# Normalisation in the projection: epsilon added on GpSimd, row 3 normalised as one piece before row 1's softplus, row 1 loaded after the first weight pair

## The chip, the cores and the metric

The kernel runs on one core of a Trainium2 chip. Its time is the device time in microseconds (us) of one execution. The engines are TensorE (PE in the profile, its weight loads PEld), VectorE (DVE), ScalarE (ACT), GpSimd (POOL) and SyncE (SP), which here only starts transfers. Each engine has a program of its own that runs in order; they wait for each other through semaphores.

## What is computed

Four rows (batch elements) of 1024 tokens with 128 channels go through a state-space layer, a mixture of experts, a long convolution and the mixture again, each with a residual. The change lies in the state-space layer's first part:

```python
def _layernorm(x, axis=-1, eps=1e-05):
    m = jnp.mean(x, axis=axis, keepdims=True)
    v = jnp.var(x, axis=axis, keepdims=True)
    return (x - m) / jnp.sqrt(v + eps)

# state-space layer, on the normalised x
x_in = x @ w_in
proj = x_in @ w_x                                  # split into dt_low, B, C
dt = softplus(dt_low @ w_dt + b_dt) * (DT_MAX - DT_MIN) + DT_MIN
# scan over tokens t:  h = exp(dt*A)*h + (dt*A . B)*x_in ;  y = h . C + Dp*x_in
```

## The kernel before

The kernel is in stages; the first two matter here. `project` normalises the tokens, transposes them, multiplies them by folded weights and makes for each row the inputs of the scan. `scan` then runs, for each of the four rows, 16 scans of 128x1024 on VectorE (L786), with ScalarE making the decays ahead of each (L780) and GpSimd multiplying 15 of the 16 results by C (L924; the tenth is multiplied by VectorE). The mixtures and the convolution follow.

In `project` the unit of work is half a row, called (b, q): four tiles of 128 tokens of row b. For each half:

- SyncE loads x. Rows 0 and 1 come in halves (L249), rows 2 and 3 whole (L253). Between row 0 and row 1 SyncE waits until the three weights w_x, w_dt and b_dt have landed (`weights_in`). ScalarE has started five small transfers before: w_in and the identity, which count on `first_in`, and then those three.
- `statistics_of(b, q)` on VectorE: four `bn_stats` (L471), a drain, four `bn_aggr` (L474), which leave mean and variance, a drain, and one 128x4 `tensor_scalar` (L476), which adds epsilon to the variances and releases GpSimd.
- `deviation(b, q)` on GpSimd: one 128x4 `tensor_tensor` with the power -0.5 (L309), which gives 1/sqrt.
- `normalize(b, q)` on VectorE: four 128x128 `tensor_scalar` (L482), each (x - mean) * rstd from SBUF to SBUF.
- TensorE transposes the tiles (L605), ScalarE copies them out of PSUM (L349), TensorE multiplies them by four weights: the step's z (L613), u (L618), B (L625) and C (L632). ScalarE takes Abs of z (L356) and copies the others; VectorE's `positive(b, q)` (L489) takes max(z, 0) out of PSUM and so frees z's bank for the next half.

For each whole row, ScalarE makes ln(1 + exp(-|z|)) (L373, L377). VectorE's `softplus(b)` (L496) adds it to the positive part; both its inputs lie in SBUF. The step is then split into three bfloat16 parts: ScalarE casts the first (`first_part`, L382), GpSimd's `remainder(b)` (L305, 128x1024) subtracts it, ScalarE casts the second (L386), VectorE's `third_part(b)` (L508) takes the rest. VectorE's `step_times_u(b)` (L503, two SBUF inputs) makes dt*u, TensorE multiplies it by the rates (L642, `step_products`), and VectorE's `input_rows(b)` (L514) makes the scan's input. `rates()` (L525 to L530) makes the rates once, `constants()` (L518 to L521) the bfloat16 tables, `skip_diagonal()` (L535) a 128x128 `tensor_scalar` from SBUF to SBUF.

The order on every engine is written out by hand. VectorE's, from the middle: softplus(0), positive(1,0), statistics_of(3,0), statistics_of(3,1), constants, step_times_u(0), third_part(0), positive(1,1), normalize(3,0), rates, softplus(1), positive(2,0), normalize(3,1), step_times_u(1), skip_diagonal, positive(2,1), input_rows(0), third_part(1), softplus(2), and so on to the first scans. GpSimd's: six deviations, remainder(0), deviation(3,0), deviation(3,1), remainder(1), remainder(2). After normalize(0,1) VectorE also has a run of semaphore increments for the later stages (`more_credit`, L115).

Of the kernel before, what the change touches and what calls it, by code (L numbers as in the profile page):

```python
# [20 lines left out]
ALU = mybir.AluOpType  # L21
# [3 lines left out]
P = 128  # L25
# [18 lines left out]
EPS = 1e-5  # L44
# [148 lines left out]
def project(plan, ps, m, t):  # L193
# [22 lines left out]
    spread, rstd = sb("in_spread", [P, 2, HT]), sb("in_rstd", [P, 2, HT])  # L216
    m["scratch"] = scratch = sb("scratch", [P, 2 * SEQ])
    xn, xn_t = (scratch[:, i * SEQ:(i + 1) * SEQ].rearrange("p (q s) -> p q s", q=2) for i in range(2))
    a_neg = sb("a_neg", [P, STATES])
    a_range = sb("a_range", [P, P])  # L220
    a_p = sb("a_p", [P, GROUPS])
# [24 lines left out]
    @plan.on("sync")  # L246
    def _(sp):
        def half_row(b, q):
            sp.dma_start(x[:, b * BT + q * HT:b * BT + (q + 1) * HT, 0:D],  # L249
                         t["x"][b, q * HALF:(q + 1) * HALF, :].rearrange("(i p) d -> p i d", p=P)).then_inc(x_in[2 * b + q], 16)  # L250

        def row(b):
            sp.dma_start(x[:, b * BT:(b + 1) * BT, 0:D], t["x"][b, :, :].rearrange("(i p) d -> p i d", p=P)).then_inc(x_in[b + 2], 16)  # L253

        half_row(0, 0)
        half_row(0, 1)
        sp.wait_ge(weights_in, 16 * 3)
        half_row(1, 0)
        half_row(1, 1)
        row(2)  # L260
        sp.dma_start(const[:, P:], t["table"][:, P:]).then_inc(consts_in, 16)
        row(3)
        sp.dma_start(a_neg[:, :], t["a_A_log"]).then_inc(a_in, 16)
        sp.dma_start(a_p[:, :], t["a_A_log_p"]).then_inc(a_in, 16)
        sp.dma_start(m["skip"][:, :], t["a_Dp"].rearrange("(d o) -> d o", o=1)).then_inc(m["skip_in"], 16)
        sp.dma_start(m["w_r_raw"][:, :], t["f_Wr"]).then_inc(m["router_in"], 16)
        sp.dma_start(m["b_r"][:, :], t["f_br"].rearrange("(o e) -> o e", o=1).broadcast_to([P, EXPERTS])).then_inc(m["router_in"], 16)

        sp.wait_ge(zero_made, 1 + CREDIT)

        def clear(dst, b):
            sp.dma_start(dst[b * SEQ:(b + 1) * SEQ, :].rearrange("(p j) d -> p (j d)", p=P), zero[:, :]).then_inc(m["prepared"], 16)

        sp.dma_start(m["taps"][:, :], zero[0:1, 0:4 * P]).then_inc(m["prepared"], 16)
        for b in range(BATCH):

            if b < BATCH - 1:
                need(sp, lo_done, b + 1)
            else:
                need(sp, last_lo, 2)  # L280
            sp.dma_start(m["steps"][:, b * PARTS * SEQ:(b + 1) * PARTS * SEQ], part[:, :]).then_inc(steps_out, 16)
            sp.wait_ge(steps_out, b * 16 + 16)
            sp.sem_inc(parts_free, 1)
            for a in range(PARTS):
                sp.dma_start(stack[a * QUARTER:(a + 1) * QUARTER, :, b * SEQ:(b + 1) * SEQ],
                             m["steps"][:, (b * PARTS + a) * SEQ:(b * PARTS + a + 1) * SEQ].rearrange(
                                 "(q r) s -> r q s", r=QUARTER)).then_inc(stacked[b], 16)
        for dst in m["slots"]:
            for b in range(BATCH):
                clear(dst, b)  # L290
        sp.wait_ge(m["prepared"], PREPARED)
        need(sp, inp_done, BATCH)

    @plan.on("gpsimd")
    def _(pool):
        pool.memset(m["neg_half"][:, :], -0.5).then_inc(half_made, 1)
        pool.memset(m["ones"][:, :], 1.0)
        pool.memset(zero[:, :], 0.0).then_inc(zero_made, 1)
        pool.wait_ge(half_made, 1 + CREDIT)

        def remainder(b):

            pool.wait_ge(hi_done, b + 1 + CREDIT)
            need(pool, lo_done, b)
            pool.tensor_tensor(rest[:, :], sp_all[:, b * SEQ:(b + 1) * SEQ], part[:, 0:SEQ], ALU.subtract).then_inc(rest_done, 1)  # L305

        def deviation(b, q):
            pool.wait_ge(moments_done, 2 * b + q + 1 + CREDIT)
            pool.tensor_tensor(rstd[:, q, :], spread[:, q, :], m["neg_half"][:, 0:HT], ALU.pow).then_inc(rstd_done, 1)  # L309

        deviation(0, 0)
        deviation(0, 1)
        deviation(1, 0)
        deviation(1, 1)
        deviation(2, 0)
        deviation(2, 1)
        remainder(0)
        deviation(3, 0)
        deviation(3, 1)
        remainder(1)  # L320
        remainder(2)
        late["gpsimd"] = {0: lambda: (need(pool, dtu_done, BATCH), need(pool, lo_done, BATCH - 1))}
# [144 lines left out]
    def _(dve):  # L467
        def statistics_of(b, q):
# [2 lines left out]
                dve.bn_stats(stats[:, q, i, :], x[:, b * BT + q * HT + i, 0:D])  # L471
            dve.drain()
            for i in range(HT):
                dve.bn_aggr(moments[:, q, i, :], stats[:, q, i, :])  # L474
            dve.drain()
            dve.tensor_scalar(spread[:, q, :], moments[:, q, :, 1], EPS, None, ALU.add).then_inc(moments_done, 1)  # L476

        def normalize(b, q):
            dve.wait_ge(rstd_done, 2 * b + q + 1 + CREDIT)
# [79 lines left out]
        third_part(0)  # L559
        positive(1, 1)  # L560
        normalize(3, 0)
        rates()
        softplus(1)
        positive(2, 0)
        normalize(3, 1)
        step_times_u(1)
        skip_diagonal()
        positive(2, 1)
# [1711 lines left out]
```

## Time and profile before

| | us |
|---|---|
| median of 3 runs | 469.01 |
| lowest, highest | 466.15, 469.39 |
| the profiled execution's own time | 466.43 |
| its span, first to last instruction | 464.6 |
| VectorE busy in the span | 333.3 (72%) |
| GpSimd busy | 290.2 (62%) |
| TensorE busy | 350.6 (75%) |
| ScalarE busy | 232.9 (50%) |

Times in the profile count from the span's start. A row of a timeline gives start, duration, engine, line, operation, output<-inputs and the number of instructions merged into it; a bracket gives the idle time before it and what ended it. Two VectorE rows that follow without a wait overlap by about 0.08 us in such a view, so what an instruction costs its engine is the distance between two starts.

### The profile page before, as it was taken

To read this page: it belongs to the slowest core of one execution; us is meant where nothing else is said; L and a number is where in the kernel's file an instruction comes from. 1 tells how busy PE (TensorE), PEld (TensorE's weight loads), DVE (VectorE), ACT (ScalarE), POOL (GpSimd) and SP (SyncE) were. 2 spreads that over 40 slices of the span, in tenths; PEclk is the share of its full clock that TensorE was granted. 3 is DMA by queue.
4 is the path that set the end of the run, shared out by engine and by line. 5 is a ranking of instruction groups with operands and counts; after the bars stand their busy time and mean duration, and the time that the engine had idled before them with its cause. 6 is when DMAs were issued, how large, how long until landed. Compare 5 with 4: busy or idle time off the path is not lost.

```text
span 464.6 us, 5440 instructions
## 1 busy us (share of the span) xinstructions
PE 350.6 (75%) x1552; PEld 178.2 (38%) x1552; DVE 333.3 (72%) x772; ACT 232.9 (50%) x383; POOL 290.2 (62%) x203
## 2 busy tenths in 40 slices
PE   4988658769967957969574787287899677688792
PEld 3433213315313403424122554135666655344441
DVE  5999999999999999986433765353869845355341
ACT  3888856556556466533121495044796111346440
POOL 3331497999999999955744000867637565426755
PEclk9999968985967888897767799589599998699987
DMA  6214420784100100101313251111302121132201
GB/s 168 83 70 136 137 66 7 231 309 128 45 0 2 45 1 1 45 4 39 98 36 107 80 161 69 46 34 37 89 0 65 41 79 60 35 126 80 64 15 33
DMA packets 28826, 33.37 MB, mean 72 GB/s; under 512 B 5357, under 2 KB 20737, under 8 KB 28796
## 3 DMA queue, kind: packets, MB, share of 16 engines
q1 hardware_dynamic: 24428, 25.96, 18.0%
q0 software_dynamic: 3712, 6.84, 4.8%
q8 instruction: 13, 0.21, 0.2%
q10 hardware_dynamic: 656, 0.21, 0.2%
q14 instruction: 17, 0.14, 0.1%
HBM read 14.23 MB, written 19.65 MB: 73 GB/s over the span
## 4 chain that ended last, share of the span: by engine, by line
issue 26%; PE 26%; DVE 26%; ACT 9%; another core or an unknown queue 4%; DMA 3%; DVEq 3%; POOL 1%; ACTq 0%; SPq 0%; POOLq 0%
DVE states L786 14%; PE ps L1834 2%; ACT scaled L1393 2%; PE ps L1920 2%; PE ps L1345 2%; PE ps L1073 2%; PE ps L1613 2%; DVE scratch L482 2%; PE ps L153 2%; PE ps L1191 2%; PE ps L1329 1%; PE ps L1909 1%; ACT ps L780 1%; POOL x L1289 1%
## 5 line engine op out<-in xcount | busy, mean ns | idle before, releaser
L924 POOL TENSOR_TENSOR states<-states,c_rows 128x1024 f32<-128x1024 f32 x60 | 142.6, 2410 | 9.2 <-DVE dtu L503 5.1
L786 DVE TENSOR_TENSOR_SCAN states<-ps,inp 128x1024 f32<-128x1024 f32 x64 | 140.5, 2264 | 0.6 <-ACT ps L780 0.5
L780 ACT ACTIVATE ps<-ps,bias_p,scale_p 128x1024 f32<-128x1024 f32 x64 | 75.0, 1177 | 57.0 <-PE ps L774 57.0
L1165 POOL DMA_INDIRECT slots<-x,put x56 | 54.7, 977 | 43.8 <-DVE put L1159 28.8
L774 PE MATMUL ps<-stack,sel 96*128 96x512 bf16 x128 | 47.7, 466 | 28.9 <-DVE states L786 27.4
L1289 POOL DMA_INDIRECT x<-answers,put x28 | 27.3, 976 | 50.8 <-DMA answers<-reply 39.6
L1488 POOL DMA_INDIRECT out<-reply,home x32 | 31.8, 995 | 23.5 <-DVE reply L1465 15.9
L1465 DVE SCALAR_TENSOR_TENSOR reply<-ps,rows,kept 128x128 f32<-128x128 f32 x64 | 18.6, 344 | 26.4 <-remote 12.0
L808 PE MATMUL ps<-states,red 128*32 128x512 f32 x256 | 36.2, 673 | 0.2 <-POOL states L924 0.2
L774 PEld LDWEIGHTS ps<-stack,sel 96*128 96x128 bf16 x128 | 9.7, 107 | 64.8 <-DVE states L786 54.2
L1861 DVE SCALAR_TENSOR_TENSOR c_s<-c_u,c_w_tap,c_s 128x1024 f32<-128x1024 f32 (+1 forms) x20 | 20.6, 1068 | 13.0 <-ACT c_s L1851 11.4
L1008 DVE BATCH_NORM_STATS2 stats<-x 128x6 f32<-128x128 f32 x96 | 19.8, 279 | 10.8 <-DMA x<-answers,put 9.7
L1624 PE MATMUL ps<-d_hidden,w 128*128 128x512 f32 x32 | 21.0, 742 | 3.2 <-ACT d_hidden L1582 3.2
L1345 PE MATMUL ps<-w,hidden 128*128 128x128 f32 x112 | 16.2, 288 | 7.5 <-ACT hidden L1407 6.4
L1613 PE MATMUL ps<-d_rows_t,w 128*128 128x512 f32 x32 | 20.7, 735 | 1.5 <-ACT d_hidden L1582 0.8
L1582 ACT ACTIVATE d_hidden<-ps,b 128x512 f32<-128x512 f32 x16 | 11.0, 685 | 21.4 <-PE ps L1616 10.3
L153 PE MATMUL ps<-ones 128*128 128x512 bf16 x69 | 19.6, 431 | 2.2 <-POOL states L924 1.4
L305 POOL TENSOR_TENSOR rest<-states,part 128x1024 f32<-128x1024 f32 x3 | 6.5, 2178 | 20.6 <-ACT part L382 20.6
L1017 ACT ACTIVATE rstd<-moments,eps 128x8 f32<-128x8 f32 (+1 forms) x13 | 3.9, 298 | 30.8 <-DVE moments L1011 24.2
L1834 PE MATMUL ps<-c_xt,c_w_in 128*128 128x512 f32 x32 | 17.4, 670 | 2.1 <-ACT c_xt L1199 1.3
L1451 DVE SCALAR_TENSOR_TENSOR kept<-b,rows 128x128 f32<-128x128 f32 x64 | 18.2, 345 | 0.6
L1345 PEld LDWEIGHTS ps<-w,hidden 128*128 128x128 f32 x112 | 13.5, 191 | 12.7 <-ACT hidden L1407 10.3
(207 smaller groups left out, 675.7 us busy)
## 6 DMA issues: line engine op xcount, KB each, us to landing
slots<-zero SPq DMA_DIRECT2D x8, 528.0 KB
rows<-slots SPq DMA_DIRECT2D x16, 264.0 KB
steps<-part SPq DMA_DIRECT2D x4, 768.0 KB, 3.3
stack<-steps SPq DMA_DIRECT2D x12, 256.0 KB, 4.1
answers<-x SPq DMA_DIRECT2D x4, 512.0 KB, 3.2
answers<-reply SPq DMA_DIRECT2D x8, 256.0 KB, 3.2
out<-x SPq DMA_DIRECT2D x3, 512.0 KB
x<-in_x SPq DMA_DIRECT2D x4, 256.0 KB, 3.1
```

Source lines behind the costliest of these rows:

```text
L153: pe.matmul(bank(ps, at), m["ones"][:, :], ones, start=True, stop=True)
L774: last = pe.matmul(bank(ps, slot(b, u) + q), sel[0:PARTS * QUARTER, (g % QG) * P:(g % QG + 1) * P], stack[:, g // QG, bass.ds(b * SEQ + q ...
L780: act.activation(bank(ps, slot(b, u), 2), bank(ps, slot(b, u), 2), ACT.Exp, scale=m["scale_p"][:, group(u):group(u) + 1], bias=m["bias_p"] ...
L786: dve.tensor_tensor_scan(h[:, u * SEQ:(u + 1) * SEQ], bank(ps, slot(b, u), 2), inp[:, b * SEQ:(b + 1) * SEQ], 0.0, ALU.mult, ALU.add).then ...
L808: last = pe.matmul(ps[c * QUARTER:(c + 1) * QUARTER, (6 + q) * HALF:(7 + q) * HALF], red[:, r * QUARTER:(r + 1) * QUARTER], h[:, (QUARTERS ...
L924: eng.tensor_tensor(h[:, u * SEQ:(u + 1) * SEQ], h[:, u * SEQ:(u + 1) * SEQ], c_rows[:, b * SEQ:(b + 1) * SEQ], ALU.mult).then_inc(done, 1)
L1165: pool.indirect_dma_start(out=m["slots"][n // BATCH], out_offset=bass.IndirectOffsetOnAxis(m["put"][:, b, i:i + 1], 0), in_=m["x"][:, b * ...
L1289: pool.indirect_dma_start(out=m["x"][:, b * BT + i, 0:D], out_offset=None, in_=m["answers"], in_offset=bass.IndirectOffsetOnAxis(m["put"][ ...
L1345: last = pe.matmul(ps[:, at + j * D:at + (j + 1) * D], m["hidden"][:, e % 2, j * P:(j + 1) * P], m["w2"][:, e, :], start=True, stop=True)
L1488: pool.indirect_dma_start(out=m["out"], out_offset=bass.IndirectOffsetOnAxis(m["home"][:, e, j:j + 1], 0), in_=m["reply"][:, e, j * D:(j + ...
L1613: pe.matmul(at, self.m["w1"][:, e, :], self.rows_t[:, half], start=True, stop=False)
L1834: pe.matmul(bank(self.ps, self.U + s), self.w_in[:, s, :], self.xt[:, b % 2, h * HALF:(h + 1) * HALF], start=True, stop=True).then_inc(sel ...
```

## The change

1. The epsilon: `statistics_of` loses its second drain and the `tensor_scalar` of L476; the last `bn_aggr` releases GpSimd itself. `deviation` on GpSimd gets a 128x4 `tensor_tensor` add of the variances and a tile filled with epsilon, and a drain, ahead of the power. A 128x4 memset of that tile comes first in GpSimd's program.
2. VectorE's order: `normalize(3, 1)` stands directly behind `normalize(3, 0)`, ahead of `rates`, `softplus(1)` and `positive(2, 0)`.
3. SyncE starts row 1's loads once w_in and the identity have landed, and no longer waits for the three later weights.

```diff
+    in_eps = sb("in_eps", [P, HT])
...
-        sp.wait_ge(weights_in, 16 * 3)
+        sp.wait_ge(first_in, 16 * 2)
         half_row(1, 0)
...
+        pool.memset(in_eps[:, :], EPS)
         pool.memset(m["neg_half"][:, :], -0.5).then_inc(half_made, 1)
...
         def deviation(b, q):
             pool.wait_ge(moments_done, 2 * b + q + 1 + CREDIT)
+            pool.tensor_tensor(spread[:, q, :], moments[:, q, :, 1], in_eps[:, :], ALU.add)
+            pool.drain()
             pool.tensor_tensor(rstd[:, q, :], spread[:, q, :], m["neg_half"][:, 0:HT], ALU.pow).then_inc(rstd_done, 1)
...
             for i in range(HT):
-                dve.bn_aggr(moments[:, q, i, :], stats[:, q, i, :])
-            dve.drain()
-            dve.tensor_scalar(spread[:, q, :], moments[:, q, :, 1], EPS, None, ALU.add).then_inc(moments_done, 1)
+                last = dve.bn_aggr(moments[:, q, i, :], stats[:, q, i, :])
+            last.then_inc(moments_done, 1)
...
         normalize(3, 0)
+        normalize(3, 1)
         rates()
         softplus(1)
         positive(2, 0)
-        normalize(3, 1)
         step_times_u(1)
         skip_diagonal()
```

## Rows read from the trace of the kernel before

**Rows 1.** Busy time by stretch: PE, PEld, DVE, ACT, POOL busy (instructions), clock, DMA share, GB/s

```profile
24.00:39.00 15.00, 13.38 (x37) 5.47 (x35) 14.22 (x38) 13.33 (x24) 6.66 (x4) 1.00 0.36 107
55.30:199.00 143.70, 112.62 (x530) 43.63 (x530) 143.41 (x71) 82.89 (x83) 139.53 (x59) 0.80 0.23 74
```

**Rows 2.** DVE's waits from 55 to 200 us: total, times, longest

```profile
DVE states L786 <- ACT ps L780: 0.5, 2, 0.2
```

**Rows 3.** Timeline of DVE, one statistics call's tail and the next call

```profile
16.80 0.38 DVE L474 BATCH_NORM_AGGREGATE in_moments<-in_stats 128x2 f32<-128x6 f32 x4
17.26 0.17 DVE L476 TENSOR_SCALAR in_spread<-in_moments 128x4 f32<-128x4 f32 x1
17.34 0.86 DVE L471 BATCH_NORM_STATS2 in_stats<-x 128x6 f32<-128x128 f32 x4
```

**Rows 4.** Timelines of DVE and POOL around GpSimd's first two remainders

```profile
24.08 2.13 POOL L305 TENSOR_TENSOR rest<-states,part 128x1024 f32<-128x1024 f32 x1 [3.97 <-ACT part L382]
24.89 1.34 DVE L476 TENSOR_SCALAR in_spread<-in_moments 128x4 f32<-128x4 f32 x1
...
35.65 2.27 POOL L305 TENSOR_TENSOR rest<-states,part 128x1024 f32<-128x1024 f32 x1 [6.61 <-ACT part L382]
35.84 2.16 DVE L482 TENSOR_SCALAR scratch<-x,in_moments,in_rstd 128x128 f32<-128x128 f32 x1
```

**Rows 5.** Timelines of DVE and POOL where DVE reads two SBUF inputs

```profile
78.70 1.20 DVE L924 TENSOR_TENSOR states<-states,c_rows 128x1024 f32<-128x1024 f32 x1
78.86 3.24 POOL L924 TENSOR_TENSOR states<-states,c_rows 128x1024 f32<-128x1024 f32 x1 [2.24 <-DVE states L786]
...
350.88 2.11 DVE L1150 SCALAR_TENSOR_TENSOR x<-x,moments 128x8 f32<-128x8 f32 x1
```

**Rows 6.** POOL's groups by line and shape: busy us, mean ns, idle before

```profile
L924 POOL TENSOR_TENSOR states<-states,c_rows 128x1024 f32<-128x1024 f32 x60 | 142.6, 2410 | 9.2 <-DVE dtu L503 5.1 <-DVE states L786 3.9
...
L309 POOL TENSOR_TENSOR in_rstd<-in_spread,neg_half 128x4 f32<-128x4 f32 x8 | 8.6, 1075 | 12.0 <-DVE in_spread L476 11.9
...
L296 POOL MEMSET neg_half<- 128x32 f32 x1 | 0.1, 125 | 0.7 <-POOLq L2262 0.7
```

**Rows 7.** Timeline and chain that ended last, first 14 us

```profile
5.07 0.17 DVE in_spread L476
...
6.79 1.09 POOL in_rstd L309
...
10.15 0.88 DVE L471 BATCH_NORM_STATS2 in_stats<-x 128x6 f32<-128x128 f32 x4 [1.12 <-issue]
...
13.15 1.11 DVE L482 TENSOR_SCALAR scratch<-x,in_moments,in_rstd 128x128 f32<-128x128 f32 x4
```

**Rows 8.** Transfers: SyncE's third start of x, and the page's landing time

```profile
6.11 0.37 SPq L249 DMA_DIRECT2D x<-in_x  x1
...
x<-in_x SPq DMA_DIRECT2D x4, 256.0 KB, 3.1
```

**Rows 9.** Timelines of ACT and DVE: Abs of (1,0), positive(1,0), logarithm of row 1

```profile
21.57 0.72 ACT L356 ACTIVATE states<-ps,b_dt 128x512 f32<-128x512 f32 x1
22.84 0.74 DVE L489 TENSOR_SCALAR states<-ps,b_dt 128x512 f32<-128x512 f32 x1
...
30.34 1.06 ACT L377 ACTIVATE states<-states 128x1024 f32<-128x1024 f32 x1
```

**Rows 10.** Timeline of DVE and ACT from softplus(1) to positive(2,1)

```profile
33.27 1.22 DVE L496 TENSOR_TENSOR states<-states 128x1024 f32<-128x1024 f32 x1
...
34.52 1.05 ACT L382 CAST part<-states 128x1024 bf16<-128x1024 f32 x1
...
38.15 1.23 DVE L503 SCALAR_TENSOR_TENSOR dtu<-states,u 128x1024 f32<-128x1024 f32 x1 [0.16 <-issue]
...
39.30 0.28 DVE L535 TENSOR_SCALAR diag<-const,skip 128x128 f32<-128x128 f32 x1
39.49 0.74 DVE L489 TENSOR_SCALAR states<-ps,b_dt 128x512 f32<-128x512 f32 x1
```

## The prediction

> **What bounds the kernel now.** I read the busy time by stretch first. From 24 to 39 us VectorE is busy 14.2 of 15 us and ScalarE 13.3; from 55.3 to 199 us VectorE is busy 143.4 of 143.7 and GpSimd 139.5 [rows 1]. VectorE's waits in that second stretch come to 0.5 us in all [rows 2]. So VectorE sets the pace from the projection to the end of the scans, and GpSimd runs close behind it: a time at which the scans begin earlier is handed on to everything behind them. The question is only when the second scan starts, and that is a matter of the first 55 us.
>
> The second view is the timeline of VectorE in the projection. It has hardly an idle moment, but two instructions are far too long [rows 4]. The 128x4 `tensor_scalar` of L476 takes 1.34 us at 24.89, where the same one takes 0.17 at 17.26 [rows 3]; it ends when GpSimd's remainder(0) does (24.08 + 2.13 = 26.21). The last 128x128 piece of normalize(3,1) takes 2.16 us at 35.84 and ends with remainder(1) (35.65 + 2.27 = 37.92). These are the two stalls of this stage, 1.17 and about 1.8 us. One more sentence on who wins: the GpSimd instruction began at 35.65, when three of the four pieces were out or running, and the fourth, started 0.08 us before the third ended, lost to it. A waiting GpSimd gets in between two back-to-back VectorE instructions.
>
> The third view is the pair in which VectorE reads two SBUF inputs [rows 5]. GpSimd's product at 78.86 takes 3.24 us beside a VectorE product that started at 78.70 and lasts 1.20, against a mean of 2.41 [rows 6]; and a 128x8 instruction of VectorE takes 2.11 at 350.88 while GpSimd is at work. So not only `tensor_scalar` from SBUF, but also softplus, step_times_u and third_part exclude GpSimd, and are excluded by it. Instructions that read PSUM (`positive`, `input_rows`, the scans) and the `bn_` ones run beside GpSimd at their usual length.
>
> **Part 1, the epsilon: what VectorE saves.** With its second drain and L476 a call goes from the start of `bn_aggr` at 16.80 to the next instruction at 17.34, 0.54 us. Without them the next one can follow `bn_aggr` as others follow without a drain: 0.38 - 0.08 = 0.30 [rows 3]. That is 0.24 us for each of eight calls, 1.9 in all, if nothing else holds VectorE.
>
> **What GpSimd pays.** Call the step from the add's start to the power's start A. The trace has no 128x4 add. From below: memset of 128x32, 0.13 us. From above: the 128x4 power, 1.08. The 1024-column product takes 2.41 [rows 6]; that is 2.35 ns a column if nothing is fixed, and a fixed part of 1 us would leave 1.4 ns. I take a fixed part of 0.2, nearest to the memset, and 0.1 for the drain (a drained step of VectorE opens a gap of about 0.08 [rows 3]): A = 0.3, with ends 0.15 and 1.1.
>
> The Trainium skill (GPSIMD Engine Reference, Elementwise side-by-side) gives 4497 ns for a 2048-column add on GpSimd; as an estimate, a line through that figure and the 2.41 us of the 1024-column rows here has 0.3 us at zero columns, which makes A 0.4 with the drain and the gain below some 0.3 smaller. No row here shows the small add.
>
> **Stretch by stretch, with A = 0.3.** *To 10 us.* The second power is on the chain: it ends at 7.88 and normalize(0,1) follows [rows 7]. Afterwards the variances of (0,0) are released by `bn_aggr` at 5.00, GpSimd starts at 5.07, and does (0.3 + 1.02) twice with one hand-over: 7.7. Gain 0.1 to 0.2. Behind it come 2 us of VectorE's semaphore increments, which shift with it: statistics_of(1,0) at 10.0, before 10.15. *To 21 us.* normalize(1,0) waits for the power: 10.0 + 0.95 (four `bn_stats`, 0.88 [rows 7], and the drain) + 0.38 (`bn_aggr`) + 0.08 + 0.3 + 1.02 = 12.7, before 13.15: gain 0.4. The calls for row 2 add 0.48, since their powers finish just ahead of their use: VectorE is about 0.8 early at softplus(0). *At 22 us* ScalarE catches it: Abs of (1,0) ends at 22.29 and is not moved, since ScalarE was busy without a gap before it, and positive(1,0) started at 22.84 [rows 9]. Only 0.55 to 0.65 survives. *At 25 us.* The calls for row 3 add 0.48, and the 1.17 stall on L476 goes; but remainder(0), which hangs on ScalarE's cast and so is only 0.3 earlier (23.8), still runs until 25.9, and the next instruction of its kind is the first cast of constants(), at 25.3: it waits about 0.5 for GpSimd. Together: VectorE is 0.6 + 0.5 + 1.2 - 0.5 = 1.8 early at step_times_u(0). There GpSimd's four small instructions compete with VectorE's casts and products; 0.1 lost: 1.7.
>
> **Part 2, the moved half.** It adds its undisturbed 1.02 us ahead of rates and softplus(1), which starts at 33.27 - 1.7 + 1.0 = 32.6 [rows 10]; ScalarE's logarithm ends at 31.40 [rows 9], so it isn't late. Now call softplus(1)'s end T (before: 34.49). ScalarE's cast takes it from T + 0.03 to T + 1.08, and remainder(1) asks at T + 1.16, as before. On VectorE, positive(2,0) (0.74, begun 0.08 before T) runs to T + 0.66 and step_times_u(1) from T + 0.8 to T + 2.05. It reads two SBUF inputs, so GpSimd waits, and enters at T + 2.05. Right behind it stands skip_diagonal (0.28 us [rows 10]), a `tensor_scalar` from SBUF: by the pattern of rows 4 it loses and waits until T + 4.05. positive(2,1) starts at T + 4.0, where it would start at T + 2.15. So the stall isn't removed, it moves to skip_diagonal: 1.85 instead of 1.8. With T at 33.8, positive(2,1) is at 37.8, before 39.49: 1.7 early. remainder(1) ends 0.7 later after T than it did, and third_part(1), two instructions further, is later than that. TensorE's step_products(0) waits for the moved rates, and ends at about T + 0.74, just before step_times_u(1) needs its bank.
>
> The Trainium skill (SBUF — State Buffer, on the two separate sides) has the same as a rule: the pair of ports is an exclusive lock for the whole instruction, against VectorE instructions with two SBUF inputs too. By that rule the trace agrees (rows 5), and it speaks against this move; the sum above rests on the rows.
>
> **Part 3, the loads.** Row 1's third transfer starts at 6.11 and lands about 3.1 later, 9.2 [rows 8]; statistics_of(1,0) starts at 10.15 behind VectorE's own issue, not the data [rows 7]. Starting it 0.7 earlier gains nothing; the cover is 0.9 us. The SyncE transfers behind it move 0.7 up too, and none of them is waited for. The extra memset (0.1) is over long before the first power. Zero.
>
> **Sum.** From positive(2,1) to the second scan VectorE runs without a gap, and the ScalarE and TensorE work beside it hangs on positive(2,1) and shifts with it. About 1.8 us early (1.7 to 1.9) at the second scan, and then to the end. The profiled execution: 466.4 - 1.8 = 464.6. The median lies 2.6 above that execution, so from the median the sum gives 467.2. Since one of the three runs was as low as that execution, I predict 466.8, just under the second sum.
>
> **The rivals.**
>
> *A. GpSimd's add is dear.* At A = 0.5 normalize(0,1), normalize(1,0) and both halves of row 2 wait for GpSimd, and 1.0 of the gain goes; at A = 0.6 nothing is left. At A = 1.1, the power's price, two steps are 2.2 longer before 8 us, one 0.8 at (1,0), two for rows 2: about 5.5 more, minus what the 1.8 gives: 3.5 to 4 slower, 470.5 to 473. For it: the power shows that 4 columns can cost 1.08. Against: 1024 columns cost only 2.41.
>
> *B. The stall doesn't move.* If skip_diagonal slips in ahead of GpSimd, 0.4 more is won (the end is then ScalarE's and the remainder's): -2.3; if step_times_u and GpSimd don't exclude each other and no cast waits, -3.2: 463.2 to 466. Against: rows 4 and 5.
>
> *C. The gain is given back at the scans.* GpSimd, TensorE at its lower clock (the granted clock is 0.80 in 55 to 199 us [rows 1]) or a transfer sets the start of some later stage at its old time: 0 to 0.5 gained, 468.8. Against: VectorE has 0.5 us of waits there.
>
> *D. Other stages come out otherwise.* The three runs differ by 3.2 us with the same program; a luckier or unluckier run of TensorE's clock behind 55 us gives 463 or 470 with the mechanism intact.
>
> **How the numbers follow.** The forecast (1 to 2.3 earlier) 0.58; A 0.12, a third of it beyond 1% slower; B 0.10; C 0.12; D 0.08, both ways. 1% (4.7 us) is about what a measurement of this kernel tells from no change. Faster by over 1%: part of B and of D with a low median, 0.12; slower: 0.07; within 0.81. The range takes 466.2, the lowest run, less 1.8 and some of B (463.3), and reaches up to the first part of A (469.8).
>
> **What would show it.** VectorE: `bn_aggr` to the next instruction 0.30; constants' first cast about 0.5 instead of 0.22; skip_diagonal about 2.1 long and normalize(3,1) four pieces in 1.1. GpSimd: eight adds of 0.2; remainder(1) close to 3 us with its wait. positive(2,1) near 37.8, the second scan near 53.5 instead of 55.3. The prediction is wrong if adds take 0.5 or more, if skip_diagonal is short, or if VectorE meets ScalarE's waits between 40 and 55 us.

## The result, and the profile after

| | median of runs | lowest to highest | runs | profiled execution | its span |
|---|---|---|---|---|---|
| kernel before, first shown | 469.01 us | 466.15 to 469.39 | 3 | 466.43 | 464.6 |
| kernel before, beside the changed one | 468.18 | 464.74 to 471.33 | 23 | | |
| changed kernel | 468.47 | 459.39 to 473.92 | 23 | 473.92 | 472.1 |

(The three runs of the first row are among the 23 of the second.) The ratio of the two is 0.9896 with a 95% interval of 0.9863 to 0.9930, but it leaves out each run that lies more than 1.5% above the fastest of its kernel, and since the changed kernel scatters twice as widely (standard deviation 4.3 us against 1.8), that leaves out 15 of its 23 runs and none of the other's. Over all runs the medians differ by +0.3 us and the means by -0.2 (95% interval -2.0 to +1.7). I read the result by these: no change that can be measured. What is seen is the wider scatter, and it is wider downwards too: the fastest runs of the changed kernel are 459.4 and 460.2, those of the kernel before 464.7 and 465.4. No profile of such a fast run exists. The profiled execution is the changed kernel's slowest of 23, while that of the kernel before lies in its lower quarter; so the two traces can be compared stretch by stretch, but the difference of their spans (+7.5 us) is not the effect of the change.

VectorE's timeline of the changed kernel, three stretches (start us, duration, line and operation, out<-in, count, idle before and what ended it):

```profile
9.79 0.98 DVE L475 BATCH_NORM_STATS2 in_stats<-x 128x6 f32<-128x128 f32 x4 [0.68 <-issue]
...
22.79 0.75 DVE L492 TENSOR_SCALAR states<-ps,b_dt 128x512 f32<-128x512 f32 x1 [0.35 <-ACT states L360]
...
25.60 0.38 DVE L478 BATCH_NORM_AGGREGATE in_moments<-in_stats 128x2 f32<-128x6 f32 x4
25.90 0.57 DVE L521 CAST tri<-const 128x128 bf16<-128x128 f32 x1
...
30.19 2.13 DVE L485 TENSOR_SCALAR scratch<-x,in_moments,in_rstd 128x128 f32<-128x128 f32 x8
...
32.95 1.23 DVE L499 TENSOR_TENSOR states<-states 128x1024 f32<-128x1024 f32 x1
...
35.00 1.23 DVE L506 SCALAR_TENSOR_TENSOR dtu<-states,u 128x1024 f32<-128x1024 f32 x1 [0.16 <-PE ps L645]
36.14 2.16 DVE L538 TENSOR_SCALAR diag<-const,skip 128x128 f32<-128x128 f32 x1
38.22 0.74 DVE L492 TENSOR_SCALAR states<-ps,b_dt 128x512 f32<-128x512 f32 x1
...
54.06 4.46 DVE L789 TENSOR_TENSOR_SCAN states<-ps,inp 128x1024 f32<-128x1024 f32 x2
```

GpSimd's timeline of the same execution:

```profile
5.25 0.20 POOL L311 TENSOR_TENSOR in_spread<-in_moments,in_eps 128x4 f32<-128x4 f32 x1 [2.92 <-DVE in_moments L478]
5.58 1.04 POOL L313 TENSOR_TENSOR in_rstd<-in_spread,neg_half 128x4 f32<-128x4 f32 x1
...
24.25 2.13 POOL L307 TENSOR_TENSOR rest<-states,part 128x1024 f32<-128x1024 f32 x1 [4.29 <-ACT part L386]
...
35.33 2.88 POOL L307 TENSOR_TENSOR rest<-states,part 128x1024 f32<-128x1024 f32 x1 [4.77 <-ACT part L386]
```

The epsilon costs GpSimd 0.20 us, and the power starts 0.33 after it. On VectorE `bn_aggr` at 25.60 is followed after 0.30 by the first cast, which takes 0.57 where it took 0.22, because remainder(0) runs to 26.38. The second half of row 3 is normalised in one go (2.13 for eight pieces), so the stall of [rows 4] on L482 is gone from there, and it is back in full on skip_diagonal: 2.16 us for an instruction of 0.28 [rows 10]. It began 0.09 us before the end of step_times_u(1) and still lost to remainder(1), which had been held from 35.33 and is 2.88 us long instead of 2.27. The second scan starts at 54.06, before at 55.27: 1.2 us earlier. The scans end at 198.00 (the memset behind the last of them), before at 198.88.

Behind them it goes otherwise. The longest of VectorE's waits between 199 and 262 us in the changed kernel, with the product it waits for and the late start of ScalarE that follows:

```profile
238.81 0.27 PE L1735 MATMUL ps<-mlp_col,c_w 64*64 64x1 f32 x2
...
243.76 0.15 DVE L1770 TENSOR_TENSOR mlp_col<-ps,c_b 64x1 f32<-64x1 f32 x1 [10.38 <-remote]
...
248.01 0.69 ACT L1585 ACTIVATE d_hidden<-ps,b 128x512 f32<-128x512 f32 x1 [3.66 <-remote]
```

In the kernel before, VectorE's instruction waited 1.67 us, and started 0.04 us after its product's end. Here the product ended at 239.08, so VectorE started 4.7 us after it was there. ScalarE's `d_hidden` at 248.01 is the same: its product ended at 240.45 and the last reader of its buffer at 242.81, ScalarE's own last instruction at 244.35. In the kernel before VectorE had instead seven idle gaps of 0.5 to 1.2 us between 231.5 and 238.7 us, which the changed kernel lacks; so at the first `mlp_col` the changed kernel is 7.9 us ahead (232.36 against 240.24), and loses that and more. The next work on the path, x at L1552, starts at 254.94 instead of 250.50. TensorE waits for that `d_hidden` until 248.75. By the stretches, it was granted 0.50 of its clock (1.2 GHz) throughout 245 to 255 us in the changed kernel, and 1.00 (2.4 GHz) at 245 to 250 in the kernel before, where it had worked without a pause from 240 to 248:

```profile
245.00:250.00 5.00, 1.67 (x4) 0.50 (x2) 0.28 (x1) 0.69 (x1) 0.32 (x1) 0.50 0.45 132
250.00:255.00 5.00, 4.83 (x17) 3.56 (x16) 0.06 (x1) 0.58 (x1) 0.00 (x0) 0.50 0.42 126
```

(Columns as in [rows 1].) That makes its last three groups of products about 2.07 us each instead of 1.15.

### The profile page after: what moved, and what is told of

Read it like the earlier page. It is cut to its first block, busy times and chain, and to the rows that moved or that the text cites. A ratio compares the mean times of both kernels' runs of the same rounds, so it can differ in the third digit from the quotient of the medians.

```text
span 472.1 us, 5441 instructions
## 1 busy us (share of the span) xinstructions
PE 357.7 (76%) x1552; PEld 183.2 (39%) x1552; DVE 331.2 (70%) x764; ACT 232.9 (49%) x383; POOL 292.9 (62%) x212
## 4 chain that ended last, share of the span: by engine, by line
PE 30%; DVE 24%; issue 21%; ACT 9%; another core or an unknown queue 8%; DVEq 3%; DMA 2%; POOL 1%; ACTq 1%; POOLq 0%
DVE states L789 13%; PE ps L1837 2%; PE ps L153 2%; PE ps L1348 2%; PE ps L1923 2%; PE ps L1627 2%; ACT scaled L1396 2%; PE ps L1076 2%; PE ps L1194 2%; DVE stats L1011 2%; PE ps L1339 1%; PE ps L1332 1%; PE ps L1912 1%; PE ps L1616 1%
## 5 line engine op out<-in xcount | busy, mean ns | idle before, releaser
L783 ACT ACTIVATE ps<-ps,bias_p,scale_p 128x1024 f32<-128x1024 f32 x64 | 75.0, 1177 | 57.3 <-PE ps L777 56.9
L1864 DVE SCALAR_TENSOR_TENSOR c_s<-c_u,c_w_tap,c_s 128x1024 f32<-128x1024 f32 (+1 forms) x20 | 20.6, 1067 | 13.0 <-ACT c_s L1854 11.4
L153 PE MATMUL ps<-ones 128*128 128x512 bf16 x69 | 20.9, 453 | 1.5 <-ACT c_u L1845 0.8
```

What stands on the lines that cost most here:

```text
L153: pe.matmul(bank(ps, at), m["ones"][:, :], ones, start=True, stop=True)
L783: act.activation(bank(ps, slot(b, u), 2), bank(ps, slot(b, u), 2), ACT.Exp, scale=m["scale_p"][:, group(u):group(u) + 1], bias=m["bias_p"] ...
```

## The experiments

Each kernel ran beside the kernel before on the same chip. "Difference" is that of all runs: of medians, and of means with its 95% interval (by resampling the runs; with 10 to 13 runs it is somewhat too narrow). The ratio is that with outliers left out. The last columns are from the profiled executions: the second scan's start, the idle time before the second `mlp_col` of VectorE near 233 to 245 us, what lies between the end of the scans and the end of the span, and, as "products", the time from TensorE's first products from w_b (near 10.5 us) to its next ones. In between lie four pairs of 128x512 products.

| kernel | median (runs) | median of before | difference: medians; means | ratio | second scan | mlp_col | behind the scans | products |
|---|---|---|---|---|---|---|---|---|
| before | | | | | 55.27 | 1.67 | 265.7 | 3.90 |
| after | 468.47 (23) | 468.18 | +0.3; -0.2 (-2.0 to 1.7) | 0.9896 (0.9863 to 0.9930) | 54.06 | 10.4 | 274.1 | 4.38 |
| e1 after again | 472.84 (12) | 470.47 | +2.4; +2.0 (-0.5 to 4.4) | 0.9962 (0.9918 to 1.0005) | 54.36 | 10.4 | 275.9 | 4.53 |
| e2 after, code padded | 471.31 (13) | 470.47 | +0.8; +1.5 (0.0 to 3.1) | 1.0027 (0.9995 to 1.0059) | 54.97 | 11.8 | 278.1 | 5.27 |
| e3 before, code shifted | 471.99 (12) | 470.47 | +1.5; +1.2 (-0.4 to 2.9) | 1.0034 (0.9999 to 1.0070) | 56.44 | 2.5 | 269.1 | 4.78 |
| e4 diagonal later | 472.57 (12) | 470.47 | +2.1; +1.7 (-0.2 to 3.5) | 1.0022 (0.9985 to 1.0058) | 52.82 | 10.5 | 273.4 | 3.45 |
| e5 epsilon alone | 475.58 (10) | 469.94 | +5.6; +4.3 (2.1 to 6.4) | 1.0032 (0.9985 to 1.0080) | 55.75 | 11.9 | 274.3 | 4.41 |
| e6 move alone | 471.27 (10) | 469.94 | +1.3; +0.8 (-1.3 to 2.8) | 1.0035 (0.9993 to 1.0078) | 55.49 | 3.1 | 263.7 | 4.23 |
| e7 add twice | 473.69 (10) | 469.94 | +3.8; +3.5 (1.8 to 5.2) | 1.0061 (1.0025 to 1.0097) | 55.42 | 11.9 | 274.8 | 5.37 |
| e8 after, delayed | 469.70 (10) | 469.94 | -0.2; +0.6 (-1.4 to 2.7) | 0.9994 (0.9954 to 1.0034) | 56.37 | 12.6 | 274.1 | 5.48 |
| e9 after, padded again | 445.01 (12) | 445.47 | -0.5; -0.8 (-2.0 to 0.4) | 0.9975 (0.9942 to 1.0009) | 54.35 | 4.0 | 245.5 | 4.80 |
| e10 before, with adds | 444.98 (12) | 445.47 | -0.5; -0.5 (-1.4 to 0.5) | 0.9990 (0.9961 to 1.0019) | 56.55 | 4.0 | 242.3 | 5.05 |
| e11 after a third time | 467.22 (12) | 467.77 | -0.6; interval too wide | 0.9926 (0.9882 to 0.9971) | 53.75 | 8.2 | 267.9 | 3.99 |
| e12 diagonal later again | 469.31 (12) | 467.77 | +1.5; interval too wide | 1.0002 (0.9959 to 1.0045) | 53.12 | 10.4 | 273.7 | 3.87 |

(In the last two the kernel before had one run of 566 us, which spoils its mean; without that run the means differ by -1.2 and +1.5.) The kernels were measured in five batches, each on one chip: the first, e1 to e4, e5 to e8, e9 and e10, e11 and e12. The one with e9 and e10 ran 5% faster as a whole, the kernel before too, although its chip bears the same number as that of e5 to e8; so these two are compared with each other and with the kernel before of that batch alone.

The changed kernel was compared with the kernel before three times (after, e1, e11). The mean of the three differences of means, weighted by their errors and without the run of 566 us, is 0.0 us (-1.2 to 1.3; -1.6 to 1.8 if the batches are allowed to differ). A gain of 1.8 us lies outside the one and at the edge of the other.

**How fast the first products are.** A pair of these products takes 1.02 us and follows the last after 0.86 in stretches where the granted clock is 1.00; in e4 all four do, and "products" is 3.45. In the others the first one to three pairs are longer, up to 1.92 us, near the 2.07 that such a pair takes where 0.50 is granted (248.75 us above). The granted clock reads 1.00 up to 14 us in all these profiles, so that it is TensorE's clock is read from the lengths alone. Where "products" is large, ScalarE gets z late, and VectorE waits for it at positive(0,0): 0.64 us in e3 and 0.82 in e2, nothing in the kernel before. From there on the delay stays: e3 is the kernel before but for idle drains, and its second scan comes 1.2 us later, as much as the whole difference between before and after. Two single profiles therefore give the gain only where "products" agrees: before and e11 (3.90, 3.99) give 1.5 us, before and after 1.2, e3 and after 2.4.

**The same kernel again, and two with shifted code.** The question was the 10.4 us wait. e1 repeats the changed kernel. e2 puts 16 drains at the head of VectorE's work, e3 puts 17 at the head of GpSimd's work in the kernel before.

```
e2:  +        for _ in range(16):
     +            dve.drain()
e3:  +        for _ in range(17):
     +            pool.drain()
```

> The changed kernel once more, to see which of its numbers repeat. Theory (the gain lies in the projection and is about 1.2 to 1.8 us; what the whole execution shows beyond it comes from the stages behind 200 us): the second scan starts at 53.5 to 54.2 again, skip_diagonal takes about 2.1 us, the adds 0.2; the executions spread over more than 8 us. Rival (the change itself moves the later stages by a fixed amount): the time from the last scan's start to the end is within 1 us of what it was in the first profile of the changed kernel (276 us).

> The changed kernel with 16 drains at the head of VectorE's program, where it waits for x anyway; they put back the 16 instructions that the change takes out of VectorE's code, and cost nothing on the way. Theory A (the wider spread of the changed kernel's executions comes from where VectorE's code lies, so where it is fetched): the spread goes back to that of the kernel before, about 6 us, and the median lies 1 to 2 us below it. Theory B (the spread has nothing to do with the code's place): the same wide spread as the changed kernel in this call. Either way the second scan starts at 53.5 to 54.2.

> The kernel before with 17 drains in GpSimd's program behind its memsets, where it waits for VectorE until 5.4 us; they shift GpSimd's later code as the change does (8 adds, 8 drains, 1 memset). Theory A' (the place of GpSimd's code makes the spread): a spread as wide as the changed kernel's. Theory B: the spread and the median of the kernel before. The second scan at 55.2 to 55.5 either way.

The wait came back in e1 to the tenth (10.4) and in e2 (11.8), and not in e3. So it isn't an accident of one execution, and 16 more instructions ahead on VectorE don't remove it. That the place of the code does it was not borne out. On the scatter, which e2 and e3 were made for: the standard deviations are 4.3 us in e1, 2.6 in e2, 2.6 in e3 and 2.5 for the kernel before. So the padded kernel scatters like the kernel before, as theory A had it, but its median is not below it; with 12 and 13 runs, and 2.5 us in the unpadded e7, that is a hint and no proof. Shifting GpSimd's code (theory A') did nothing. The second scans missed what was expected: e1 by 0.2 us, e2 by 0.8, e3 by 0.9, all later, with long "products".

At one other place the padding is seen. The idle time that the profile calls "issue" before statistics_of(1,0), behind VectorE's semaphore increments, is 0.68 us in all eight changed kernels without padding (after, e1, e4, e5, e7, e8, e11, e12) and 1.11 to 1.13 in the four in which VectorE has its old instructions (before, e3, e6, e10), and in the two padded ones (e2, e9: 1.12 and 1.11). So 16 instructions ahead of it are worth 0.44 us there; why, no run shows.

**The stall taken from skip_diagonal.** e4 is the changed kernel with that call two lines further down, behind third_part(1).

```
         positive(2, 1)
         ...
         third_part(1)
+        skip_diagonal()
```

> The changed kernel with skip_diagonal moved behind third_part(1). Theory (the stall moved from normalize(3,1) to skip_diagonal, because VectorE's SBUF instruction is held while GpSimd's remainder runs): skip_diagonal takes 0.3 us, positive(2,1) starts 1.3 to 1.4 us earlier after softplus(1) than in the changed kernel (3.9 instead of 5.3), but third_part(1) waits for ScalarE's cast of the remainder, which began 0.7 us late behind step_times_u(1), so only 0.4 us reach the second scan (53.6). Rival 1 (skip_diagonal is long for a reason of its own, such as its transfer): it still takes 2.1 us at its new place. Rival 2 (all of the 2 us come through): the second scan starts near 52.2.

VectorE's timeline of e4:

```profile
32.18 1.23 DVE L499 TENSOR_TENSOR states<-states 128x1024 f32<-128x1024 f32 x1
...
34.23 1.23 DVE L506 SCALAR_TENSOR_TENSOR dtu<-states,u 128x1024 f32<-128x1024 f32 x1 [0.16 <-PE ps L645]
36.08 0.75 DVE L492 TENSOR_SCALAR states<-ps,b_dt 128x512 f32<-128x512 f32 x1 [0.62 <-ACT states L360]
...
38.56 1.22 DVE L511 TENSOR_TENSOR part<-rest,part 128x1024 bf16<-128x1024 f32 x1 [0.60 <-ACT part L390]
39.70 0.28 DVE L538 TENSOR_SCALAR diag<-const,skip 128x128 f32<-128x128 f32 x1
```

skip_diagonal is short again, which shows that GpSimd's remainder is what held it. But of its 1.9 us two waits of 0.6 for ScalarE come back: first for its |x| of (2,1), then for the cast that itself waits for the remainder. From softplus(1) to the second scan it is 20.6 us instead of 21.1: half a microsecond. (Its second scan, 52.82, is earlier by more, for its "products" are the shortest of all.)

**The parts one by one.** e5 is the changed kernel without the moved line and the load's new condition; e6 is the kernel before with the moved line alone; e7 writes each sum twice on GpSimd (the second writes the same values); e8 adds six `bn_stats`, whose results are not read, behind step_times_u(3).

```
e5:  -        normalize(3, 1)          (ahead of rates)
     +        normalize(3, 1)          (where it was)
e6:  +        normalize(3, 1)          (ahead of rates, nothing else changed)
e7:  +            for _ in range(2):
                      pool.tensor_tensor(spread[:, q, :], moments[:, q, :, 1], in_eps[:, :], ALU.add)
                      pool.drain()
e8:  +        for i in range(6):
     +            dve.bn_stats(stats[:, i // HT, i % HT, :], x[:, 3 * BT + i, 0:D])
```

> The kernel before with the epsilon on GpSimd alone: normalize(3,1) stays behind positive(2,0), row 1 loads behind the three weights. Theory (the move only moves a stall, so nearly all of the projection's gain is the epsilon's): the fourth piece of normalize(3,1) takes about 2.1 us again, and from softplus(1)'s start to the second scan it is 22.1 to 22.3 us (before: 22.0; changed: 21.1), while softplus(1) starts at 31.9 to 32.2 instead of 33.0; the second scan is 0.2 us behind the changed kernel's, at 54.2 to 54.4 for the same rise of TensorE's clock. Rival (the move is worth the 1.8 us stall): the second scan at 55.3 or later.

> The kernel before with normalize(3,1) moved ahead of rates, and nothing else. Theory: skip_diagonal takes about 2.1 us in place of 0.28, the tensor_scalar of L476 keeps its 1.34 us, and the second scan starts at 55.1 to 55.5, 0.2 earlier than before at most. Rival (the move is worth the stall): the second scan near 53.5.

> The changed kernel with GpSimd's add and drain done twice in each deviation, the same values written again. A goes from 0.33 to 0.67. Theory (the power's chain through GpSimd is waited for in five places up to softplus(0), so A counts several times): normalize(0,1) 0.7 later, normalize(1,0) 1.0, normalize(2,0) 1.3, and the second scan 1.8 to 2.0 later than the changed kernel's, at 55.8 to 56.2. Rival (GpSimd's part is hidden beside VectorE's work): less than 0.7 later.

> The changed kernel with six more 128x128 bn_stats on VectorE (unused results) behind step_times_u(3), 1.2 us, so that the second scan starts when it did before. In all four profiles of the changed kernel and its variants VectorE waits 10 to 12 us for a small product of the convolution's filter near 233 us (L1767 of the kernel before) and its expert stage begins 4 us late; in both profiles of the kernel before it waits 1.7. Theory T (that wait comes from when the scans end, against the fetching and the clock around 200 us): it is gone here, and the stretch from the last scan's end to the execution's end is 266 to 269 us as in the kernel before. Theory C (it comes from something else in the changed kernel, such as its code or its memory): it stays at 10 us, and the stretch stays at 274 to 278 us.

*e5.* positive(2,1) starts at 38.28, with the move at 38.22 (after) and 38.51 (e1): up to there the move is worth 0.2 us at most (counted from the first `bn_stats`), as expected. Then e5 missed its expectation by 1.4 us. Its stretches and VectorE's row say why:

```profile
40.00:42.00 2.00, 2.00 (x3) 0.67 (x2) 1.91 (x3) 1.36 (x3) 0.00 (x0) 0.50 0.00 0
42.00:44.00 2.00, 2.00 (x5) 0.90 (x4) 1.27 (x2) 1.26 (x3) 0.00 (x0) 0.70 0.97 393
```

```profile
44.65 1.22 DVE L517 TENSOR_TENSOR inp<-inp,ps 128x1024 f32<-128x1024 f32 x1 [1.38 <-PE ps L645]
```

TensorE had been without work from 37.5 to 39.17 and fell to 1.2 GHz at about 39.8; step_products(1) was then late, and VectorE waited 1.38 us for it. Without that wait the second scan would be at 54.4, as expected. In the changed kernel that pause is 0.87 us, and the clock stayed at 1.00. In the kernel before it is 1.68 without a fall, so the pause alone doesn't decide, and whether the move protects from the fall is not shown by one execution. e5 is also the slowest by its runs (+4.3 us in the mean of all runs, clear of noise; the ratio with outliers left out shows none of it), with 8.6 us more behind the scans than before; what in it does that is open. And since e5 has the loads where they were, and its statistics_of(1,0) starts 6.03 us after the first `bn_stats` against 6.02 in the changed kernel, the earlier loads are worth nothing.

*e6.* softplus(1) at 34.45, skip_diagonal 2.15 at 37.64, second scan at 55.49 (expected 55.1 to 55.5): moved but not removed, with no gain. *e7.* The step from the first sum to the power is 0.68 us instead of 0.33, softplus(0) 1.9 later than in the changed kernel, the second scan at 55.42, where the kernel before had 55.27. That looks as if at 0.68 the whole gain were gone. But e7's "products" is 5.37, and VectorE waits 0.40 us for ScalarE at positive(0,0), where its own work was done. With the products of the kernel before, e7 would stand at 54.9 to 55.0 by my estimate from these rows, so 0.3 to 0.5 us of the gain is left; against e3, the kernel before with late products (56.44), it is 1.0. The second scan is later than the changed kernel's by 1.1 to 1.4 instead of the 1.8 to 2.0 expected: VectorE then no longer waits for ScalarE at positive(1,0) (0.35 in the changed kernel), and less for remainder(0) at the first cast (0.46 instead of 0.57). *e8.* VectorE is 2.3 us later at the scans (1.2 by the `bn_stats`, 1.1 by late products), and the wait is still there, 12.6: the moment at which the stages behind the scans begin doesn't decide either. (The 1.7 us that its expectation gives for both profiles of the kernel before are 1.7 and, in e3, 2.5.)

**The other kernel with sums, and another padding.** e9 is the changed kernel with eight pairs of a drain and a 128x4 memset at the head of VectorE's work; e10 is the kernel before in which GpSimd also makes the eight sums, into a tile that nobody reads.

```
e9:  +        for _ in range(8):
     +            dve.drain()
     +            dve.memset(pad[:, :], 0.0)
e10: +            pool.tensor_tensor(idle_sum[:, q, :], moments[:, q, :, 1], in_eps[:, :], ALU.add)
     +            pool.drain()
```

> The changed kernel with eight pairs of a drain and a 128x4 memset at the head of VectorE's program, where it waits for x: 16 instructions again, but half of them are real ones, as the eight drains and eight tensor_scalars were that the change takes out. In the profiles so far every kernel with the epsilon on GpSimd, wherever its scans end (196.5 to 200.3 us), has a wait of 10 to 12.6 us of VectorE for the filter's small product near 233 us, and none without it has. Theory V (it hangs on where VectorE's later code lies; drains alone may not move it): the wait is gone, under 2 us, and the median is 1 to 3 us lower than the changed kernel's. Theory G (it comes from GpSimd's adds): the wait stays at 10 us or more. The projection as in the changed kernel: second scan at 54.0 to 55.0.

> The kernel before with GpSimd's eight adds, drains and the memset, whose sums nobody reads; VectorE keeps its drain and tensor_scalar. Theory V: no long wait near 233 us, the spread of the kernel before. Theory G: the wait of 10 us or more is there. The projection: A is paid and nothing is saved on VectorE, so the second scan starts 1.5 to 2.5 us later than before, at 56.8 to 57.8.

Neither has the wait of 10 us (4.0, for TensorE's product, in both). But this batch was another in all: the same stages behind the scans took 245.5 and 242.3 us, at least 18 less than in any other profile. So the missing wait can't be laid to the kernels, and the test does not decide. What it gives is the projection: e10's second scan, with the sums' price and nothing saved, is at 56.55, a little ahead of the 56.8 to 57.8 expected, and e9's at 54.35, as expected, is 2.2 ahead of it. Of the 1.3 us by which e10 lies behind the kernel before, 0.24 is a later first `bn_stats` and 0.41 a wait for ScalarE at positive(0,0) behind late products, so that the eight sums alone cost about 0.6, less than was expected.

**Once more, with and without the stall.**

> The changed kernel once more, beside the kernel before. Theory P (the projection's gain is real and reaches the end unless something behind 200 us takes it back): softplus(1) at 32.5 to 33.4 us, skip_diagonal 2.16 us, second scan 1.0 to 1.6 us ahead of the kernel before, and, where no wait of 10 us or more stands at mlp_col near 233 us, a time 0.5 to 2 us below the kernel before. Rival G (the epsilon on GpSimd brings that wait with it): the wait of 10 to 12 us is there and the time is equal or up to 4 us above. Rival N: the time differs from the kernel before by under 0.5 us although the wait is absent, so the gain is given back elsewhere.

> The changed kernel with skip_diagonal() behind third_part(1), once more and beside the changed kernel. Theory (the stall of 1.9 us on skip_diagonal is exchanged for two waits of 0.6 us): from softplus(1) to the second scan 20.3 us instead of 21.1, second scan 0.6 to 1.0 us earlier than in the changed kernel, skip_diagonal 0.28 us. In the time 0.4 to 1.0 us below the changed kernel, if the end follows the projection; equal to it within 0.3 us, if stages behind it set the end anyway. Rival: the waiting subtraction of GpSimd stalls another VectorE operation of that stretch by about 2 us, and nothing is gained.

e11 is the one profiled execution of the changed kernel that stands at its median (467.23 against 467.22). The wait is 8.2 us, its second scan 53.75, the scans end at 197.50, and its span is 465.4. e12 repeats e4: its second scan comes 0.6 earlier than e11's, its scans end 0.5 earlier, and in the time nothing of it is seen (2.1 above e11 by the medians, with 9 to 11 us from the lowest to the highest run of each). From softplus(1) to the second scan e12 takes 20.6 us, as e4 did; the 20.3 in its expectation was a misreading of e4.

**What the runs say of the wait.** In the four batches at 468 to 470 us all nine profiles with the sums on GpSimd show 8.2 to 12.6 us at `mlp_col`, and 267.9 to 278.1 us behind the scans; the three without (before, e3, e6) show 1.7 to 3.1 us, and 263.7 to 269.1. The runs' times follow this only in part: the medians of the nine lie 0.6 below to 5.6 above the kernel before, those of e3 and e6 1.5 and 1.3 above it. Nearer to the wait the line between the two kinds is sharp. In all nine, VectorE starts 3.3 (e11) to 7.1 us (e8) after the end of the product it waits for; in the other five profiles, e9 and e10 among them, 0.04 us after it. ScalarE's last `d_hidden` of this stage is preceded by 1.6 to 4.3 us of idle time in the nine and by 0.79 in the five. The three without the sums have instead a string of idle "issue" gaps of VectorE between 229 and 239 us, which none of the nine has. From the end of the scans to x at L1552 it takes 51.6 to 52.2 us in the three, 56.9 to 58.6 in the nine and 41.3 in e9 and e10. So in each of the nine profiles 5 to 7 us are lost here, more than the projection gained, and a varying part comes back behind x: e11's stages behind x are 3.1 us shorter than those of the kernel before.

The profile names the releaser "remote" or "issue": no engine of this core is seen to be late, and two engines start late with their inputs there. The kernel before has waits of that kind too, at other places (4.5 us before L1549, 5.5 at ACT L1582). Shown is that the wait is no single accident, that it is not cured by 16 drains ahead on VectorE nor by a delay of 2 us, and that it is absent in a batch in which everything behind the scans was quicker. Not tested is which half of the change brings it: each of the nine has both the sums on GpSimd and VectorE without its drain and `tensor_scalar`, and the only kernel with one and not the other, e10, ran in the quick batch. Its cause stays open.

## Why the prediction came out as it did

The forecast was no measurable change, 466.8 us with a range of 463.3 to 469.8; the runs gave 468.47. That the number fits says little: a change worth nothing would have given 468 too. The sum behind it, -1.8 us handed on to the end, came true at the scans and is not seen in the time. Step by step:

- **The add, A = 0.3.** Right: 0.33 in the trace, in the ends 0.15 to 1.1. The line drawn beside it from the Trainium skill's figure (GPSIMD Engine Reference, Elementwise side-by-side), 0.4 with the drain, lies 0.07 above what was measured. Rival A priced the add too dearly: it had nothing of the gain left at A = 0.6, and at 0.68 e7 keeps 0.3 to 0.5 us of it by the estimate above.
- **VectorE's saving.** Right: 0.30 us from `bn_aggr` to the next, the first cast 0.57 (about 0.5 forecast). One term was too small: statistics_of(1,0), forecast 0.15 us early, is 0.46 early counted from the first `bn_stats`, for the idle gap ahead of it shrank from 1.12 to 0.68 us, which the sum had at its old length. It adds little to the end, since VectorE is held by ScalarE further on.
- **Where ScalarE catches VectorE.** Right in the mechanism, and the size depends on TensorE's clock. I had taken ScalarE's |x| of (1,0) as "not moved". It was moved, by 0.47 (22.04 against 21.57), and only 0.05 of the gain survived there instead of 0.55 to 0.65. What was late is seen at TensorE, whose products from w_b change from their long to their short duration at about that time. They take 1.50 us in the kernel before; the row of the changed kernel, of e11, and of e4:

```profile
10.51 1.92 PE L628 MATMUL ps<-scratch,w_b 128*128 128x512 f32 x2
```

```profile
10.59 1.58 PE L628 MATMUL ps<-scratch,w_b 128*128 128x512 f32 x2
```

```profile
10.66 1.04 PE L628 MATMUL ps<-scratch,w_b 128*128 128x512 f32 x2
```

  The first two are the same program, and e4 differs only behind 36 us: the moment at which the products become short varies between executions. With it goes softplus(1): 32.95, 32.63 and 32.18. So of the 0.5 us that the trace of after lacks, 0.4 is no effect of the change. In e11, whose products became short nearly as in the kernel before, positive(1,0) starts 0.54 us earlier counted from the first `bn_stats` (0.55 to 0.65 forecast), softplus(1) is at 32.63 (forecast 32.6) and the second scan at 53.75 (53.5). Counted from the first `bn_stats` (3.85 against 3.67) that is 1.7 us earlier than before; the forecast was 1.7 to 1.9.
- **The moved half.** Right: one call of 2.13 instead of two, the stall of 1.85 moved to skip_diagonal (2.16 long), positive(2,1) at 38.2 in the trace of after with its late products and at 37.9 in e11, 37.8 forecast. e6 shows the same for the move alone. The Trainium skill's rule that the two engines' port pair is locked for a whole instruction (SBUF — State Buffer) agrees here too: remainder(1) was issued at 35.33 while step_times_u(1) ran, and is 2.88 us long, 0.75 more than the 2.13 of remainder(0).
- **The load.** Right: the loads of row 1 start 0.9 earlier, and statistics_of(1,0) still starts behind "issue" (9.79 [0.68 <-issue]); e5, without the earlier loads, starts it just as early.
- **Handed on to the end.** Right as far as the end of the scans: 1.2 earlier became 0.9 in after (198.00 against 198.88), 1.5 became 1.4 in e11 (197.50). Beyond it, it was only argued, from VectorE's lack of waits up to 199 us, and there it failed: I had looked at no wait behind 200 us, where VectorE, TensorE and ScalarE have idle stretches of 4 to 10 us, set neither by VectorE nor by the projection. In e11, the execution at the median, x at L1552 comes 5.3 us later behind the end of the scans than in the kernel before, and the stages behind the scans take 2.2 us more in all. The nearest rivals are C and D of the prediction, which I had given 0.20 together, though neither named this place or an amount above the gain. The 23 runs alone don't tell them from my forecast (-1.8 lies in the interval of -2.0 to 1.7); the three comparisons together speak for them.

The best of the versions by the second scan is e4 (52.82 and, in e12, 53.12), but its times are not below those of either kernel, so there is no version to put in their place.

## What to carry to other kernels

When two engines exclude each other, moving the victim out of the way only picks the next one: write down which instruction stands right behind the holder's release, and ask whether it is of the excluded kind; e4 shows that even with a free successor the waits behind it take back more than half (a stall of 1.9 us gone, 0.5 won). A gain at the head of a kernel is to be followed through every later stage, and not to the point up to which the busiest engine has no gaps. Before half a microsecond, lost or won, is put down to an edit, look at how fast TensorE's first products ran in both executions. And where an engine waits long, look at when its input was there: here the two were up to 7 us apart.

## What the runs showed of the hardware

- A GpSimd instruction that already waits gets in between two VectorE instructions although the second started 0.08 to 0.09 us before the first ended: 2.16, 2.15 and 2.16 us for an instruction of 0.28 in after, e6 and e11.
- A 128x4 addition takes GpSimd 0.20 us where a 128x4 power takes 1.01 to 1.05 undisturbed: here the operation, not the columns, makes the price.
- The moment at which TensorE's first products become short (from 1.9 us a pair to 1.02) differs between executions of one program: the first pair takes 1.92, 1.91 and 1.58 us in after, e1 and e11, and the time to the next w_b products 4.38, 4.53 and 3.99. The granted clock reads 1.00 all the while.
- TensorE's granted clock fell after a pause of 1.68 us in e5 (0.50 from 40 to 42 us), and did not after a pause of the same length in the kernel before.
- Sixteen instructions more at the head of VectorE's program lengthened an idle gap near 10 us from 0.68 to 1.12 us (e2, e9).
- One wait of 8 to 13 us, at whose end VectorE starts 3.3 to 7.1 us after its input is there, came in nine of nine profiles of one kind of kernel in four batches, and not in the one of that kind (e9) in a batch whose runs were all 5% faster. It wasn't found out why.
